# Order of the two probability transposes in a split-precision cross-attention kernel: high part of a tile ahead of the low part of the tile behind

## The reference

```python
q = (pre_q @ Wq + bq).reshape(b, ql, H, D_Q)      # pre_q (16, 100, 128)
k = (pre_k @ Wk + bk).reshape(b, kl, H, D_Q)      # pre_k (16, 1444, 128)
v = (pre_k @ Wv + bv).reshape(b, kl, H, D_Q)
attn = softmax(einsum('bqhd,bkhd->bhqk', q, k) / sqrt(D_Q), axis=-1)
ctx = einsum('bhqk,bkhd->bqhd', attn, v).reshape(b, ql, H * D_Q)
x = pre_q + ctx @ Wo + bo
out = (x - mean(x)) * rsqrt(var(x) + EPS) * gamma + beta
```

## Time and profile before

| | |
|---|---|
| median of 3 runs | 870.71 us (869.03 to 873.26) |
| profiled execution | 871.59 us, its span 869.8 us |
| granted TensorE clock | 0.998 |
| TensorE (PE) busy | 846.3 us, 97% |
| weight loads (PEld) | 605.2 us, 70% |
| ScalarE (ACT) busy | 779.6 us, 90% |
| VectorE (DVE) busy | 774.7 us, 89% |
| GpSimd (POOL) busy | 569.1 us, 65% |
| DMA | 180.80 MB, mean 208 GB/s |

### The profile page before, as it was taken

How to read it: one execution, slowest core, us unless ns; L and a number is a source line. 1 busy time by engine, 2 the same in 40 slices (tenths; PEclk the granted TensorE clock), 3 DMA queues, 4 the chain that set the end, 5 groups by cost and what they waited for, 6 DMA issues and landing times.

```text
span 869.8 us, 19632 instructions
## 1 busy us (share of the span) xinstructions
PE 846.3 (97%) x7306; PEld 605.2 (70%) x7306; DVE 774.7 (89%) x938; ACT 779.6 (90%) x1132; POOL 569.1 (65%) x575
## 2 busy tenths in 40 slices
PE   7999999999999999999999999999999999999996
PEld 6676776767677766777667776776767777677675
DVE  4988888999989989999899998999899999999984
ACT  5899999989999989999989999998989989999983
POOL 2283997949566693867749586694956669397301
PEclk9999999999999999999999999999999999999999
DMA  7899999999999999999999999999999999999985
GB/s 198 186 211 192 195 210 189 216 200 223 215 209 217 217 204 224 209 226 211 205 213 221 216 208 229 198 227 217 213 215 220 205 233 208 222 188 217 209 183 117
DMA packets 683939, 180.80 MB, mean 208 GB/s; under 512 B 654596, under 2 KB 683076, under 8 KB 683844
## 3 DMA queue, kind: packets, MB, share of 16 engines
q1 hardware_dynamic: 682372, 179.01, 105.7%
q10 hardware_dynamic: 1344, 0.53, 0.3%
q0 software_dynamic: 128, 0.01, 0.0%
HBM read 15.35 MB, written 0.82 MB: 19 GB/s over the span
## 4 chain that ended last, share of the span: by engine, by line
PE 52%; ACT 14%; DVE 13%; DMA 8%; issue 7%; SPq 4%; ACTq 0%; POOLq 0%; POOL 0%; DVEq 0%
PE ps L670 25%; PE ps L631 22%; DMA pt_hi<-p_hi 7%; DVE p_lo L932 6%; ACT p L1072 6%; ACT p_hi L1080 5%; DVE nmax L917 4%; SPq L429 2%; PE ps L495 2%; PE ps L488 2%; SPq L420 1%; ACT unused L1023 1%; DMA bq_pairs<-in_L_xattn_bq_dram 1%; DVE rsum L923 1%; ACT o_t L1110 1%
## 5 line engine op out<-in xcount | busy, mean ns | idle before, releaser
L932 DVE SCALAR_TENSOR_TENSOR p_lo<-p,rinv,p_hi 128x1444 f16<-128x1444 f32 x200 | 370.9, 1855 | 7.5 <-ACT p_hi L1080 7.0
L917 DVE TENSOR_REDUCE nmax<-ps 128x1 f32<-128x1446 f32 x200 | 330.0, 1650 | 18.8 <-PE ps L631 18.3
L1080 ACT ACTIVATE p_hi<-p,rinv 128x1444 f16<-128x1444 f32 x200 | 300.0, 1500 | 32.1 <-DVE rinv L925 28.5
L1072 ACT ACTIVATE p<-ps,nmax 128x1446 f32<-128x1446 f32 x200 | 292.2, 1461 | 17.8 <-DVE nmax L917 15.4
L670 PE MATMUL ps<-pt_hi,c_hi 128*128 128x256 f16 (+1 forms) x1232 | 252.9, 261 | 11.4 <-DMA pt_hi<-p_hi 9.0
L670 PE MATMUL ps<-pt_hi,c_lo 128*128 128x256 f16 (+1 forms) x1232 | 253.0, 261 | 0.0
L631 PE MATMUL ps<-ct_hi,g_hi 128*128 128x482 f16 (+3 forms) x624 | 155.5, 367 | 0.8 <-DVE g_lo L892 0.7
L631 PE MATMUL ps<-ct_lo,g_hi 128*128 128x482 f16 (+3 forms) x624 | 154.9, 366 | 0.0
L631 PE MATMUL ps<-ct_hi,g_lo 128*128 128x482 f16 (+3 forms) x624 | 154.9, 366 | 0.0
L670 PEld LDWEIGHTS ps<-pt_hi,c_hi 128*128 128x128 f16 x1232 | 114.1, 98 | 50.4 <-issue 16.8
L1204 POOL TENSOR_TENSOR g_raw<-g_raw,gb_b 128x400 f32<-128x400 f32 x60 | 81.0, 1350 | 96.2 <-ACT g_raw L1096 96.2
(11 more groups left out here) (138 smaller groups left out, 863.0 us busy)
## 6 DMA issues: line engine op xcount, KB each, us to landing
c_raw<-in_ctx_dram SPq DMA_DIRECT2D x32, 256.0 KB, 6.1
pt_hi<-p_hi SPq DMA_TRANSPOSE x200, 3.5
pt_lo<-p_lo SPq DMA_TRANSPOSE x200, 3.7
c_raw<-in_ctx_dram SPq DMA_DIRECT2D x16, 192.0 KB
c_raw<-in_ctx_dram SPq DMA_DIRECT2D x48, 18.0 KB
out_dram<-late_sb SPq DMA_DIRECT2D x16, 50.0 KB
x_sb<-in_x_dram SPq DMA_DIRECT2D x1, 600.0 KB
o_t<-in_L_xattn_Wq_dram SPq DMA_DIRECT2D x2, 256.0 KB, 4.5
```

The costliest lines, as they stand in the source:

```text
L917: dve.tensor_reduce(nmax[:, n % RING:n % RING + 1], ps[:, bank:bank + 3, 0:KEYW], AX.XY, ALU.max, negate=True).then_inc(s_nm, 1)
L932: dve.scalar_tensor_tensor(out=p_lo[:, n % LOS, 0:KL], in0=p32[:, n % P32S, 0:KL], scalar=rinv[:, i:i + 1], in1=p_hi[:, par, 0:KL], op0=AL ...
L1072: act.activation(p32[:, n % P32S, :].rearrange("p (k w) -> p k w", w=KEYW), ps[:, bank:bank + 3, 0:KEYW], ACT.Exp, bias=nmax[:, i:i + 1], ...
L1080: act.activation(p_hi[:, par, 0:KL], p32[:, n % P32S, 0:KL], ACT.Copy, scale=rinv[:, i:i + 1]).then_inc(s_hi, 1)
```

## The change

SyncE's loop issues the high part of tile n first and the low part of tile n - 1 behind it. The context two batches ahead comes in six pieces of two tiles at r = 0 to 5 in place of three of four tiles at r = 1 to 3, with a semaphore for each half, so that each sum of magnitudes waits for its own half. The store of a finished batch moves from r = 2 to r = 10. In the prologue TensorE builds the second two banks of A ahead of the query bias and of x; ScalarE empties all four banks ahead of its first sum (three of them before it was at the high part of the context already, the last one after that), VectorE takes over the copy of x and of the query bias. The rows of bias, gamma and beta come by transfers that spread them over all partitions, and J_R only makes the bias product, to which VectorE adds bo.

```diff
-    LOADS = 6
+    TL = 2
+    NL = KT // TL
-    LOAD_AT = 1
-    STORE_AT = 2
+    LOAD_AT = 0
+    STORE_AT = 10
...
+            def load_context(b, i):
+                load_tiles(b, TL * i, TL * (i + 1), s_c[b % 2][i * SUMS // NL])
...
             for n in range(N + 1):
+                if n < N:
+                    transpose_hi(n)
                 if n >= 1:
                     transpose_lo(n - 1)
                 if n == N:
                     break
-                transpose_hi(n)
                 w, r = window(n)
-                if LOAD_AT <= r < LOAD_AT + NT and w + 2 < B:
+                if LOAD_AT <= r < LOAD_AT + NL and w + 2 < B:
...
             head_products_by_two(w_t[0], w_t[1], 0, J_A)
+            head_products_by_two(w_t[0], w_t[1], 2, J_B)
             query_bias(take(J_X))
             spread_context_max(job_bank(J_G + 2), 0)
             transpose_x(0, J_X).then_inc(s_fill, 1)
-            head_products_by_two(w_t[0], w_t[1], 2, J_B)
...
                 for c in range(PAIRS):
-                    pe.matmul(bank[:, 0:P], bv_wide[:, c, :], wo_sb[:, c, :], start=(c == 0), stop=False)
-                pe.matmul(bank[:, 0:P], ones_row[:, :], rows_sb[:, 0, :], start=False, stop=True)
-                pe.matmul(bank[:, P:2 * P], ones_row[:, :], rows_sb[:, 1, :], start=True, stop=True)
-                pe.matmul(bank[:, 2 * P:3 * P], ones_row[:, :], rows_sb[:, 2, :], start=True,
-                          stop=True).then_inc(s_fill, 1)
+                    mm = pe.matmul(bank[:, 0:P], bv_wide[:, c, :], wo_sb[:, c, :], start=(c == 0), stop=(c == PAIRS - 1))
+                mm.then_inc(s_fill, 1)
...
-                last = copy(rows_b[:, :, :], split(bank, 3, P))
+                eng.wait_ge(s_small, 16 * 3)
+                last = eng.tensor_tensor(rows_b[:, 0, :], bank[:, 0:P], bo_b[:, :], ALU.add)
...
-            empty(J_B)
+            empty(J_X)
+            dve.tensor_scalar(gb_sb[:, :], job_bank(J_X)[:, XG * QL:XG * QL + H], SCALE, None, ALU.mult).then_inc(s_gb, 1)
...
             def context_sum(b, i):
+                act.wait_ge(s_c[b % 2][i], context_landed(b, i))
                 if i == 0:
-                    act.wait_ge(s_c[b % 2], context_landed(b))
                     act.wait_ge(s_cm, b)
...
-            for k in (1, 3, J_A, J_A + 1):
+            for k in (1, 3, J_A, J_A + 1, J_B, J_B + 1):
                 empty(k)
             a_sum(0)
-            empty(J_X)
-            act.activation(gb_sb[:, :], job_bank(J_X)[:, XG * QL:XG * QL + H], ACT.Copy, scale=SCALE).then_inc(s_gb, 1)
             for g in range(NT):
                 context_hi(0, g)
-            empty(J_B + 1)
...
-            for i, r in enumerate((bo, gamma, beta)):
-                pool.dma_start(rows_sb[:, i, :], r.rearrange("(o d) -> o d", o=1)).then_inc(s_small, 16)
+            for place, r in ((bo_b[:, :], bo), (rows_b[:, 1, :], gamma), (rows_b[:, 2, :], beta)):
+                pool.dma_start(place, r.rearrange("(o d) -> o d", o=1).to_broadcast([P, D])).then_inc(s_small, 16)
```

More of the change, by code:

```diff
@@ L174, in cross_attention_kernel @@
         g_un = sb("g_un", [P, 1])
-        rows_sb = sb("rows_sb", [1, 3, P])
-        ones_row = sb("ones_row", [1, P])
+        bo_b = sb("bo_b", [P, P])
         table = sb("table", [P, 1])
@@ L227, in cross_attention_kernel @@
         s_cf = [sem(f"first_context_loaded{g}") for g in range(NT)]
-        s_c = [sem(f"context_loaded{i}") for i in range(2)]
+        s_c = [[sem(f"context_loaded{i}_{half}") for half in range(SUMS)] for i in range(2)]
         s_bq = sem("bq_loaded")
@@ L233, in cross_attention_kernel @@
         s_part_id = sem("identity_over_range_ready")
-        s_const = sem("constants_set")
         s_id0 = sem("identity_zeroed")
@@ L309, in cross_attention_kernel @@
         s_out = [sem(f"stored{i}") for i in range(2)]
-        J_A, J_X, J_B = 4, 6, 7
-        J_G = J_B + 2
+        J_A, J_B, J_X = 4, 6, 8
+        J_G = J_X + 1
         J_V0, J_V1, J_M0, J_M1, J_M2, J_M3, J_X1, J_X2, J_X3, J_R = range(J_G + NG, J_G + NG + 10)
@@ L318, in cross_attention_kernel @@
                  J_V0: O_BANK, J_V1: O_BANK, J_M2: O_BANK, J_M3: O_BANK}
-        BY_SCALAR = [1, 3, J_A, J_A + 1, J_X, J_B + 1, J_V1, J_M2]
+        BY_SCALAR = [1, 3, J_A, J_A + 1, J_B, J_B + 1, J_V1, J_M2]
         BY_VECTOR = [k for k in range(N_PRO) if k not in BY_SCALAR]
@@ L353, in every_other, with context_landed @@
             return slice(first, first + 2 * HG - 1, 2)
-        def context_landed(b):
-            return 16 * LOADS * (b // 2 + b % 2)
+        def context_landed(b, half):
+            return 16 * (NL // SUMS + (3 if half == SUMS - 1 else 0)) * (b // 2 + b % 2)
         def emptied(eng, k):
@@ L371, in _, with load_tiles @@
         def _(sp):
[L372 to L377, removed]
+            def load_tiles(b, a, e, landed):
+                par, whole = b % 2, min(e, KT - 1)
+                sp.dma_start(c_raw[:, par, a:whole, :],
+                             ctx_in[b:b + 1, a * P:whole * P, :].rearrange("o (t p) d -> p (o t) d", p=P)).then_inc(landed, 16)
+                if e == KT:
                     tail = ctx_in[b:b + 1, (KT - 1) * P:KL, :].rearrange("o p d -> p o d")
@@ L386, in _ @@
             for g in range(NT):
-                load_context(0, g)
+                load_tiles(0, TG * g, TG * (g + 1), s_cf[g])
             sp.dma_start(x_sb[:, 0:XG, :], x[0:XG, :, :].rearrange("b q d -> q b d")).then_inc(s_x[0], 16)
@@ L391, in _ @@
                 sp.dma_start(w_raw[2][:, cols], Wv[:, cols]).then_inc(s_w[2][half], 16)
-            for g in range(NT):
-                load_context(1, g)
+            for i in range(NL):
+                load_context(1, i)
             def transpose_context_hi(b):
@@ L586, in bias_rows @@
                 bank = take(k)
-                pe.wait_ge(s_small, 16 * 3)
-                pe.wait_ge(s_const, 1)
                 pe.wait_ge(s_bvw, 1)
                 for c in range(PAIRS):
-                    pe.matmul(bank[:, 0:P], bv_wide[:, c, :], wo_sb[:, c, :], start=(c == 0), stop=False)
-                pe.matmul(bank[:, 0:P], ones_row[:, :], rows_sb[:, 0, :], start=False, stop=True)
-                pe.matmul(bank[:, P:2 * P], ones_row[:, :], rows_sb[:, 1, :], start=True, stop=True)
-                pe.matmul(bank[:, 2 * P:3 * P], ones_row[:, :], rows_sb[:, 2, :], start=True,
-                          stop=True).then_inc(s_fill, 1)
+                    mm = pe.matmul(bank[:, 0:P], bv_wide[:, c, :], wo_sb[:, c, :], start=(c == 0), stop=(c == PAIRS - 1))
+                mm.then_inc(s_fill, 1)
             def once(k):
@@ L834, in _ @@
             dve.memset(ax_parts[:, :, :], 0.0).then_inc(s_axz, 1)
-            dve.memset(ones_row[:, :], 1.0).then_inc(s_const, 1)
             def context_max(g):
-                dve.wait_ge(s_cf[g], 16 if g < NT - 1 else 16 * (LOADS - NT + 1))
+                dve.wait_ge(s_cf[g], 16 if g < NT - 1 else 16 * 4)
                 dve.tensor_reduce(c_max[:, g:g + 1], c_raw[:, 0, TG * g:TG * g + TG, :].rearrange("p t d -> p (t d)"),
```

## The result

The kernel after takes **885.75 us** (median; 882.98 to 887.28) beside 871.99 us of the kernel before: ratio **1.0158, 95% interval 1.013 to 1.0185**, slower. The forecast of 876.2 us had the direction, and its range of 863 to 888 holds the time; 13.8 us were lost where 5.5 were forecast. The profiled execution took 884.74 us, its span is 882.9 us.

What follows compares the result with a forecast made beforehand. TensorE was taken to bound the middle, with 8.5 us of idle to win. The terms -7 + 12.6 - 0.5 - 0.7 + 1.1 = +5.5 us put the median of 870.71 at 876.2 us, range 863 to 888.

Steps and rivals of the forecast that it cites:

- The low parts, +12.6: TensorE's waits for low parts: 36 of 104 units meet a fetch, 18 crowded at 0.6 us, 18 quiet at 0.1; +12.6 us.
- the 5.2 us: SyncE's queue, hi(n)'s issue to lo(n-1)'s landing: 1.42 + 0.1 + 3.7 us, in which 35% of units meet an instruction fetch.
- The 0.7: Time in us that lo(157), a crowded unit's low part, would have in hand before TensorE takes it, without a held-up issue.
- The high part's waits, -7: TensorE's idle in the middle, 8.5 us: the swap gives little, the spread loads most; -7 us, between 0 and -8.5.
- The +5 us: Extra low-part cost if a 128 KB load piece costs 0.58 us: tiles 6 and 8 to 10 run later, 0.6 becomes 0.9.
- Prologue, -0.5: Ahead of the first scores: ScalarE starts 0.65 us earlier, three broadcasts could take it all; -0.5 us, from -0.8 to +0.5.
- Bias job, -0.7: The bias job drops three products, 0.4 us each with both passes; -0.7 us, between 0 and -1.2.
- End, +1.1: At the last tiles lo(197) lands 2.0 us late, partly absorbed by the wait for hi(199); +1.1 us, between 0 and 2.0.
- A: The forecast itself: low parts become the last wait, the high part's waits go; 872 to 885 us, chance 0.5.
- B: Rival: low parts still land in time and the high part's waits go; 862 us, up to 866; chance 0.2.
- C: Rival: SyncE is the limit, issue order unchanged where it is behind, half the high part's waits stay; 868 to 873; chance 0.17.
- D: Rival: in crowded stretches every unit is late, 52 units x 0.4 us and more, +15 to +40; 886 to 910; chance 0.13.

## Why the prediction was right, and its size was not

**The low parts, +12.6: the mis-sized term.** They measured 18.8 us of waits, 16.9 without the end, which had a term of its own. The form was right: 36 units were to be late, 18 crowded by 0.6 us, 18 quiet by 0.1. Measured are 19 crowded units (one is the end's) with 1.11 us each and 4 elsewhere with 0.35. The step that failed is "without the 1.1 us that this issue took over its median it would have had 0.7 in hand. So a stall needs a held-up queue", and with it the 5.2 us in which alone a hold-up was to count. The 0.7 was read from one unit (tiles 156 and 157); its last tile is tile 7 of its window, one before the worst place. At tile 8, behind both context transposes, there is nothing in hand: with the swap alone no issue is held up in the stretch shown above, and TensorE still stands 1.14 us.

A held-up queue is nonetheless in nearly all of these waits, only further back than I looked. I counted packets of the instruction queue in the 5.2 us from hi(n)'s issue to lo(n-1)'s landing. In the kernel after, 11 of the 19 late crowded units have one there. Another 7 have none, but stand behind an issue of over 2.1 us earlier in the same unbroken row (issues less than 0.2 us apart), which runs for 11 to 43 us up to their landing: a row without gaps hands a hold-up on. The last is tile 197, at the end. So the cap of 0.9 us a unit (a hold-up of 1.6 less 0.7) fell as well; the longest is 2.7 us by the gaps. That 19 units are late where 18 were forecast is luck: 8 of the 19 crowded units that a packet met in their own 5.2 us were not late. The quiet units were read well: their median time in hand is 1.3 us, 1.7 was said, and the 4 late ones make 1.4 us of the 1.8.

**The high part's waits, -7: the size right, the cause wrong.** 9.0 fell to 1.9, -7.1. But "the swap itself gives little, and the spread of the loads gives most" is refuted: the swap alone brings 9.0 to 1.2, the loads alone to 6.0, and with both loads and prologue and the old order it is 8.2. I had argued that in a busy queue the order is hi, lo, hi, lo either way. In those places one low part fewer stands ahead of the tight high part; and each wait for a low part gives the next high part time, which the runs don't separate.

**Loads in six pieces.** A piece of 128 KB holds SyncE for 0.57 us, the upper edge, where 0.47 was taken (min/median/max):

```profile
L374 SPq DMA_DIRECT2D c_raw<-in_ctx_dram x93: 384/574/1690, 1.8 to 739.1; - x93
```

The +5 us that I had named for that don't show: the swap with the old loads loses as much (1.015 and 1.0158).

**Prologue, -0.5.** The first scores came 1.6 us later. The last third of the first context is waited for longer in the three kernels with the new prologue (2.5 to 4.1 us) than in the kernel before, in the swap alone and in the loads alone (1.4 to 2.0). In the kernel after, in order of time:

```profile
13.04 0.69 DVE L838 TENSOR_REDUCE c_max<-c_raw 128x1 f32<-128x512 f32 x1 [4.07 <-DMA c_raw<-in_ctx_dram]
...
14.71 0.16 DVE L861 RECIPROCAL alpha<-unscale 128x1 f32<-128x1 f32 x1
14.91 1.95 ACT L1015 ACTIVATE c_hi<-c_raw,alpha 128x512 f16<-128x512 f32 x3 [2.39 <-DVE alpha L861]
...
21.52 0.78 PE L629 MATMUL ps<-ct_hi,g_hi 128*128 128x482 f16 x3
```

alpha is 1.75 us later than in the earlier trace rows. If that is the price of the broadcasts, of which I said "they could take all of it" (no run has them alone), they took more than all: that edge of +0.5 was too near. ScalarE's 0.65 us between alpha and its first context part is gone, as said. In the time none of it is seen (0.999 with the new prologue alone, which also has the shorter bias job of the next paragraph). How much of the 1.6 us comes from there is open: with the same granted clock of 0.74 from 10 to 23 us the scores start at 20.19 to 21.21 in the five traces with the old prologue and at 21.27 to 22.20 in the five with the new one.

**Bias job, -0.7.** Tile 17, which carries the job J_R, takes 6.55 us from its scores to those of tile 18 in the kernel before and 5.59 in the kernel after: -1.0, inside the range. With the low parts' 18.8, the high part's -7.1 and the prologue's 1.6 that makes 12.3 of the span's 13.1.

**End, +1.1.** +1.3 from the last scores on. The wait is there, 1.88 us for the low part of tile 197; 2.0 had been worked out:

```profile
868.57 1.36 PE L668 MATMUL ps<-pt_lo,c_hi 128*128 128x256 f16 x11 [1.88 <-DMA pt_lo<-p_lo]
```

**Rivals.** The time is 0.75 us above A's 872 to 885, and A's mechanism is the one that came. B (the low part still in time) asked for 1.6 us in hand in crowded units; the median was 0.2. The price of the Trainium skill that leads to it (DMA: Bandwidth & Descriptors, "Anatomy of one DMA — SWDGE (gpsimd) path") gives 2.9 us for a low part, an estimate; after, none landed under 3.2 and the median is 3.5, so the measurement decides against it again. C (the order of issue doesn't change) asked for 4 us of waits for pt_hi; it was 1.9. D (every crowded unit late, hit or not) has its mechanism at tile 8, where 6 units of 8 were late, and not in the rest, 13 of 40.

Of the signs named ahead, pt_lo behind L668's products, mostly in tiles 8 to 12, pt_hi under 2 us and the smaller busy share of TensorE came true; the high part's issue within 0.5 us of its ready time in tiles 2 to 5 came true for 45 of 64 tiles (18 before); the one that was to speak against me, scores that start later than 19.95, came true as well and rightly marked a term that was wrong, the prologue's.

## What to carry to other kernels

In one in-order queue, moving a transfer ahead of another means that the other one's start is now tied to the first one's producer: count its time in hand from there, through everything that can stand between, and at the most crowded place of the period, not at the one that was looked at first. Where the queue stands in an unbroken row, count hold-ups over the whole row, not over the last two issues. Here the time in hand was under one step, and a whole step (a deeper pipeline) opened it; moving work within the period shifted need and supply together. Look at which of two consumers has the slack: here one tile's low part could wait almost for free and the other's could not, and the swap treated them alike.

## What the runs showed of the hardware

How long TensorE runs at the lower of its two clock levels ahead of the first scores differs from profile to profile of one and the same prologue. The granted clock from 10 to 23 us (from:to, length, PE busy, clock), in the kernel before, with the swap alone, and with the swap at a unit's second tile only:

```profile
10.00:23.00 13.00, 11.76 (x86) 0.87 0.78 192
```

```profile
10.00:23.00 13.00, 12.97 (x85) 0.74 0.77 192
```

```profile
10.00:23.00 13.00, 12.59 (x74) 0.61 0.85 189
```

The first scores start at 19.95, 20.19 and 21.57 us. In all three TensorE had been busy for 2.4 to 2.8 us of the 4 from 6 to 10 us, before the clock fell. So 1.6 us in the first 23 can't be laid on an edit from one profile each.

Slow issues and slow landings of the transposes stand beside the 16 KB packets of the instruction queue. In the kernel after, of the 400 transposes of probabilities 39 held SyncE for over 2 us; 36 of these have such a packet in their issue or in the 0.5 us ahead of it, as have 35 of the other 361. With a packet between issue and landing the median landing is 4.7 us (118 transposes), without one 3.4 (282). That the packet is the cause was not tried.
